# Attention block on one core: early scores moved to chunks 2 to 5, the last chunk and first step reordered, one fold behind the division, twelve idle matmuls at the start

## What is computed

```
q = Wq x + bq;  k = Wk x + bk        (32 channels each)
v = Wv x + bv                        (256 channels)
att = softmax(q^T k / sqrt(32))      (4096 x 4096)
out = gamma * (v att^T)
fused = Wf [out ; x] + bf            (1x1 convolution, 512 -> 256 channels)
```

## Time and profile before

| | us |
|---|---|
| median of 3 runs | 2091.38 |
| lowest, highest | 2089.87, 2096.21 |
| the profiled execution's own time | 2091.23 |
| its span in the trace | 2089.1 |
| PE busy in the span | 2040.8 |
| ACT busy | 1752.5 |
| DVE busy | 1589.7 |
| POOL busy | 1204.9 |

### The profile page before, as it was taken

One profiled execution on the slowest core, in us unless ns is written; L12 is line 12 of the kernel. 1 busy time (PEld: TensorE's weight loads), 2 busy tenths in 40 slices (PEclk: granted clock), 3 DMA queues, 4 the chain that ended last, 5 costly groups with the idle time before them and its releaser, 6 DMA issues.

```text
span 2089.1 us, 44966 instructions
## 1 busy us (share of the span) xinstructions
PE 2040.8 (98%) x16208; PEld 1992.9 (95%) x16208; DVE 1589.7 (76%) x2157; ACT 1752.5 (84%) x2373; POOL 1204.9 (58%) x514
## 2 busy tenths in 40 slices
PE   8899999999989999999999999999999999999999
PEld 7899999999889999999988999999998899999999
DVE  5788887886678788878666878887767778888885
ACT  6788888887788888888777888888877888888886
POOL 0376666677036766666703677666660466677665
PEclk9999999999999999999999999999999999999999
DMA  3200000000320000000031000000003100000000
GB/s 128 86 21 12 20 20 20 20 21 11 108 76 21 21 10 20 20 20 21 11 117 67 21 21 15 15 20 20 21 11 122 41 21 21 20 20 10 20 21 16
DMA packets 54081, 69.46 MB, mean 33 GB/s; under 512 B 4048, under 2 KB 37584, under 8 KB 53968
## 3 DMA queue, kind: packets, MB, share of 16 engines
q1 hardware_dynamic: 53696, 67.91, 10.0%
q10 hardware_dynamic: 272, 0.07, 0.0%
HBM read 34.41 MB, written 33.55 MB: 33 GB/s over the span
## 4 chain that ended last, share of the span: by engine, by line
PE 79%; issue 8%; DVE 7%; ACT 4%; DVEq 1%; DMA 0%; ACTq 0%; SPq 0%
PE ps_o L376 61%; PE ps_s L368 8%; PE ps_p L234 4%; DVE top L595 3%; PE ps_o L234 2%; ACT ps_p L529 2%; DVE o_norm L626 1%; PE ps_t L276 1%; ACT queries L466 1%; PE ps_t L234 1%; ACT hi L441 1%; PE ps_s L251 1%; PE ps_t L261 1%; PE ps_t L268 1%; DVE inv L622 1%
## 5 line engine op out<-in xcount | busy, mean ns | idle before, releaser
L736 POOL TENSOR_TENSOR raw<-raw,top_m 128x1024 f32<-128x1024 f32 x508 | 1204.2, 2410 | 868.0 <-ACT top_m L452 868.0
L614 DVE TENSOR_TENSOR lo<-ps_p,hi 128x1024 fp32r<-128x1024 f32 x512 | 626.9, 1224 | 329.7 <-ACT ps_p L529 319.3
L595 DVE TENSOR_TENSOR top<-ps_s,top 128x512 f32<-128x512 f32 x960 | 660.9, 688 | 69.6 <-ACT raw L447 14.5
L525 ACT ACTIVATE hi<-raw 128x1024 fp32r<-128x1024 f32 x512 | 543.9, 1062 | 176.7 <-PE ps_o L376 170.6
L376 PE MATMUL ps_o<-val_hi,hi 128*128 128x258 f32 x4096 | 673.7, 287 | 17.8 <-ACT hi L525 10.4
L376 PE MATMUL ps_o<-val_lo,hi 128*128 128x256 f32 x4096 | 654.5, 282 | 0.0
L376 PE MATMUL ps_o<-val_hi,lo 128*128 128x258 f32 x4096 | 602.0, 284 | 0.0
L447 ACT ACTIVATE raw<-ps_s 128x512 f32<-128x512 f32 x1024 | 554.2, 594 | 55.5 <-PE ps_s L368 32.5
L376 PEld LDWEIGHTS ps_o<-val_hi,hi 128*128 128x128 f32 x4096 | 564.6, 190 | 31.2 <-DVE o_norm L626 19.0
L376 PEld LDWEIGHTS ps_o<-val_lo,hi 128*128 128x128 f32 x4096 | 562.7, 190 | 0.0
L376 PEld LDWEIGHTS ps_o<-val_hi,lo 128*128 128x128 f32 x4096 | 541.4, 191 | 0.0
(11 more groups left out here) (63 smaller groups left out, 1029.9 us busy)
## 6 DMA issues: line engine op xcount, KB each, us to landing
xf<-x SPq DMA_DIRECT2D x32, 512.0 KB, 3.9
conv_d<-conv_st SPq DMA_DIRECT2D x64, 256.0 KB, 2.0
result<-conv_d SPq DMA_DIRECT2D x64, 256.0 KB, 2.6
out<-result SPq DMA_DIRECT2D x64, 256.0 KB, 2.2
raw<-wf2T SPq DMA_DIRECT2D x1, 256.0 KB, 4.3
raw<-wv SPq DMA_DIRECT2D x1, 256.0 KB, 4.1
raw<-wf1T SPq DMA_DIRECT2D x1, 256.0 KB, 4.9
raw<-wkqT ACTq DMA_DIRECT2D x1, 64.0 KB, 2.1
```

The costliest lines, as they stand in the source:

```text
L525: nc.scalar.activation(hi[:, p], raw[:, slot].rearrange("p j i -> p (j i)"), ACT.Exp, scale=SCALE).then_inc(hi_done, 1)
L595: nc.vector.tensor_tensor(top[:, new], scores, top[:, new if half else old], ALU.max).then_inc(max_done, 1)
L614: nc.vector.tensor_tensor(lo[:, t % 2], ps_p[:].rearrange("p h n -> p (h n)"), hi[:, t % 2].bitcast(F32), ALU.subtract).then_inc(lo_done, 1)
L736: nc.gpsimd.tensor_tensor(raw[:, slot], raw[:, slot], top_m[:, r].unsqueeze(1).broadcast_to((P, JQ, I)), ALU.subtract).then_inc(sub_done, 1)
```

## The change

- `BETWEEN` moves quads 8 to 11 from chunks 4 to 7 to chunks 2 to 5.
- Chunk 6: scores of quad 6 come directly after the values, then keys and queries of chunk 7, then the second convolution, on all three engines alike.
- Chunk 7: on PE the scores of quad 7 come first, then all four values, turning of the top, first convolution with the spreading in its middle, second convolution, now into a bank of `ps_s`. ScalarE copies that convolution between the exponentials of the first two steps. The exponential is cut into two functions.
- First block: step 0 has the order of the ordinary steps; scores of step 1 wait for that last convolution to be copied.
- Blocks 1 to 14: the second half of step 7's fold is done behind the division at step 0 of the next block.
- Chunk 0 of images 1 to 3: VectorE adds the convolution ahead of the low parts of keys and queries.
- Start: twelve matmuls of the 128x128 float32 identity on itself before the first wait for x, with a result that nobody reads; the first convolution of chunk 0 goes between `fold_weights` and the wait for `wvf_split`.

```diff
-    BETWEEN = {4: 8, 5: 9, 6: 10, 7: 11}
-    MADE = {q: k for k, q in enumerate((0, 1, 2, 3, 8, 4, 9, 5, 10, 6, 7, 11))}
+    BETWEEN = {2: 8, 3: 9, 4: 10, 5: 11}
+    MADE = {q: k for k, q in enumerate((0, 1, 8, 2, 9, 3, 10, 4, 11, 5, 6, 7))}
+
+    LAST_CONV = 2 * len(MADE) % BANKS + 2
...
+            def warm_up():
+
+                pe.wait_ge(id_made, 1)
+                for _ in range(12):
+                    nc.tensor.matmul(ps_t[:, 0:P], ident[:], ident[:], start=True, stop=True)
...
                 if last_chunk:
-                    project_values(0)
                     pe.wait_ge(k_out, C + 1)
+                    early_scores(c)
+                    for j in range(JC):
+                        project_values(j)
+                    turn_top(b * BLOCKS, None)
                     pe.wait_ge(q_out, C + 1)
-                    early_scores(c)
-                    project_values(1)
-                    convolve(ps_p[:, 0], 0)
-                    project_values(2)
-                    project_values(3)
-                    turn_top(b * BLOCKS, None)
-                    early_scores(BETWEEN[c])
-                    convolve(ps_p[:, 1], 1, lambda: spread_top(b * BLOCKS))
+                    convolve(ps_p[:, 0], 0, lambda: spread_top(b * BLOCKS))
+                    convolve(ps_s[:, LAST_CONV].rearrange("p j i -> p (j i)"), 1)
                     return
                 if start:
+                    warm_up()
                     pe.wait_ge(wkq_split, 1)
...
                 if start:
                     fold_weights()
+                    pe.wait_ge(wf2_split, 1)
+                    convolve(ps_t[:], 0)
                     pe.wait_ge(wvf_split, 1)
...
-                if c == CHUNKS - 2:
-                    project_kq(c + 1, C + 1)
                 if c in BETWEEN:
                     early_scores(BETWEEN[c])
-                convolve(ps_p[:, 1], 1)
-                early_scores(c)
+                if c == CHUNKS - 2:
+                    early_scores(c)
+                    project_kq(c + 1, C + 1)
+                    convolve(ps_p[:, 1], 1)
+                else:
+                    convolve(ps_p[:, 1], 1)
+                    early_scores(c)
...
+                    if first and t == 1:
+                        pe.wait_ge(conv_done, b * (2 * CHUNKS) + 2 * CHUNKS)
...
-                    if t == 0:
+                    if t == 0 and not first:
                         scores_ahead(t)
...
                 if last_chunk:
                     early_scores(c)
+                    conv_out(ps_p[:, 1], 1, C - 1)
                     values_out(0)
+                    values_out(1)
+                    keep_top(b * BLOCKS, 0)
                     conv_out(ps_p[:, 0], 0)
-                    values_out(1)
-                    early_scores(BETWEEN[c])
-                    keep_top(b * BLOCKS, 0)
-                    conv_out(ps_p[:, 1], 1)
-                    act.wait_ge(conv_done, C * 2 + 2)
                     act.wait_ge(sub0_done, b + 1)
-                    exponentials(b * STEPS, 0, 0)
+                    exponential_hi(0, 0)
+                    act.wait_ge(conv_done, C * 2 + 1)
+                    exponential(b * STEPS, 0, 0)
+                    conv_out(ps_s[:, LAST_CONV].rearrange("p j i -> p (j i)"), 1)
                     return
...
                 if last_chunk:
                     early_scores(c)
+                    reduce_top(b * HALVES + 2 * MADE[c] + 2)
                     values_lo(0)
-                    reduce_top(b * HALVES + 2 * MADE[c] + 2)
+                    reduce_turned(b * BLOCKS)
                     values_lo(1)
-                    reduce_turned(b * BLOCKS)
-                    early_scores(BETWEEN[c])
                     subtract_first(b * BLOCKS)
...
                 if finishing:
                     normalise(b * BLOCKS - 1, 1)
+                    add_conv(b * BLOCKS - 1, 0, b * (16 * USES[0]))
                 kq_lo(c, C)
                 if start:
                     setup_values()
-                if finishing:
-                    add_conv(b * BLOCKS - 1, 0, b * (16 * USES[0]))
...
                     if t == 0 and not first:
                         normalise(B - 1, 1)
+                        if not (isinstance(n, int) and n * QUADS + AHEAD > STEPS):
+
+                            fold_scores(H, AHEAD - 1, 2 * (QUADS * r + AHEAD - 1) % BANKS, 0, 0, (1,))
...
-                        fold_scores(H, t + AHEAD, 2 * (QUADS * r + t + AHEAD) % BANKS, old, 0)
+                        fold_scores(H, t + AHEAD, 2 * (QUADS * r + t + AHEAD) % BANKS, old, 0,
+                                    (0,) if t == QUADS - 1 else (0, 1))
```

More of the change, by code:

```diff
@@ L335, in project @@
                 project_values(1)
[L336 to L342, removed]
+                if not start:
+                    if finishing:
+                        pe.wait_ge(finished, b * BLOCKS)
+                    else:
+                        pe.wait_ge(conv_done, C * 2)
+                    convolve(ps_t[:], 0)
                 project_values(2)
@@ L468, in kq_hi, with conv_out @@
                     last.then_inc(q_hi_done, 1)
-                def conv_out(src, ot):
+                def conv_out(src, ot, C=C):
                     act.wait_ge(conv_ready, C * 2 + (ot + 1))
@@ L514, in project, with exponential_hi, exponential @@
                 values_out(1)
-                if c == CHUNKS - 2:
-                    kq_hi(c + 1, C + 1)
                 if c in BETWEEN:
                     early_scores(BETWEEN[c])
[L519 to L525, removed]
+                if c == CHUNKS - 2:
+                    early_scores(c)
+                    kq_hi(c + 1, C + 1)
+                else:
+                    conv_out(ps_p[:, 1], 1)
+                    early_scores(c)
+            def exponential_hi(t, slot):
+                nc.scalar.activation(hi[:, t % 2], raw[:, slot].rearrange("p j i -> p (j i)"), ACT.Exp,
                                      scale=SCALE).then_inc(hi_done, 1)
+            def exponential(Q, t, slot):
                 if not (isinstance(Q, int) and Q + t == 0):
@@ L543, in attend @@
                         act.wait_ge(sub_done, Q + (t + 2))
-                        exponentials(Q, t + 1, (QUADS * r + t + 1) % SLOTS)
+                        exponential_hi(t + 1, (QUADS * r + t + 1) % SLOTS)
+                        exponential(Q, t + 1, (QUADS * r + t + 1) % SLOTS)
                     elif not last_image:
@@ L583, in split_x, with fold_scores @@
                                         ALU.subtract).then_inc(x_split, 1)
-            def fold_scores(base, made, bank, old, new):
-                for half in range(2):
+            def fold_scores(base, made, bank, old, new, halves=(0, 1)):
+                for half in halves:
                     h = 2 * made + half
@@ L688, in project @@
                 values_lo(1)
-                if c == CHUNKS - 2:
-                    kq_lo(c + 1, C + 1)
                 if c in BETWEEN:
@@ L693, in project @@
                 early_scores(c)
+                if c == CHUNKS - 2:
+                    kq_lo(c + 1, C + 1)
             def attend(b, n, r, last_image):
```

## The result

| | before | after |
|---|---|---|
| median, us | 2090.62 (4 runs) | 2033.47 (4 runs) |
| lowest to highest | 2089.68 to 2096.21 | 2033.30 to 2033.55 |
| profiled execution, its span | 2091.23, 2089.1 | 2033.30, 2031.4 |

What follows compares the result with a forecast made beforehand. PE, busy 98%, bounds the kernel, so only its stops and half-clock time can pay. 22.4 + 6.3 + 15.5 + 10 + 3.1 = 57.3 off 2091.2 gives 2034 us, range 2027 to 2052.

Steps and rivals of the forecast that it cites:

- Fold behind the division: Blocks' step 0: PE's stop for o_norm goes, 56 x 0.40 = 22.4 us, bounds 11 to 24.
- Addition early: Chunk 0 of images 1 to 3: PE's 1.83 us wait for result goes, 6.3 us, bounds 0 to 6.3.
- behind 1.83 at the image starts in none: Starts of the three later images: the 1.83 us stop did not drop PE's clock in any.
- Chunks 2 to 7: Projection: shorter tail less work and waits handed to chunks 2 and 3, 15.5 us, bounds 8 to 18.
- first attention matmul within 1.0 us of the last convolution: End of each image's projection: sign that 1.0 us is left of PE's 2.62 us stop.
- The clock: Half-clock stretches behind projection stops go: 10 us, bounds 0 to 11.2; rival that it still drops: 2044, chance 0.12.
- some 0.3 per image comes back: Attention step 1: scores wait for a fold the slow clock hid, taking some 0.3 us per image off 11.2.
- Start: Kernel start: convolution fills the 1.69 us stop, half-clock stretch goes; 3.1 us, bounds 1.4 to 3.1, idle matmuls 0.
- the idle matmuls last longer: Rival, kernel start: 0.43 each, ending at 6.8, lifts the clock before real work; 2.6 us more, 2031, chance 0.17.
- another wait in the block: Rival, blocks: ScalarE or the fold is late, half or more of 22.4 gone, 2045 to 2056; 0.11 including a stop that stays.
- crowded chunks: Rival, four crowded chunks in a row: ScalarE's lag of some 1 us per chunk eats the tail's gain; 2050, chance 0.06.
- slower: Rival, blocks: VectorE at the division holds up half fold and subtraction, PE waits; 2095 at 1.1 us a block, chance 0.02.

Runs made afterwards that it cites:

- the table alone: Kernel before with only BETWEEN changed, quads 8 to 11 in chunks 2 to 5: 2092.8 us, ratio 0.9993.
- the two faster ones: Changed kernel with chunks 2 to 5's between-scores ahead of value 3: 2028.3 us; on top, chunk 7's keys' low part between quad 6's folds: 2027.6 us.
- the repeated kernel: The changed kernel itself, unaltered, run again as yardstick for later experiments: median 2033.8 us, ratio 0.9718 to the kernel before.

## Why the prediction was right, and where its steps were not

- **Fold behind the division: right.** 22.5 measured by undoing it, 22.4 forecast; the o_norm waits of PE are gone and come back with the order.
- **Addition early: right in the change, undersized when undone.** Chunk 0 of images 1 to 3 is 2.08 shorter each, 6.2 for 6.3. Undone alone it costs 10.1, as the clock then falls behind the stop. The step that failed is "behind 1.83 at the image starts in none", which I had read as a property of the stop; it was the case of one trace.
- **Chunks 2 to 7: 13.4 of 15.5.** 3.7 in image 0, and 3.3, 2.9 and 3.5 in the others with 2.1 and, in image 2, 1.7 of clock taken off. What was handed to chunks 2 and 3 came as forecast, 1.64 for 1.68. The mis-sized step is the tail from chunk 7's keys to attention, 10.9 by my times (68.50 to 79.4) in all images. It took 11.10 and 11.11 in images 0 and 3, where PE stands 0.97 and 0.88 by the starts, for 1.0 forecast, and what lies before that took 0.2 to 0.3 longer; and 11.62 and 11.70 in images 1 and 2, where the last stop is 1.24 and 1.30 instead of 0.80, and PE starts 0.59 and 0.64 behind the exponential's end, at the turn of the hardware loop. The prediction had nothing for that turn; it is half of the 2.1 that is missing, and its sign, "first attention matmul within 1.0 us of the last convolution", fails there. The working, step by step along the chain, was needed: by counting stops alone I put the table alone at 6.5, and it gave nothing.
- **The clock: right in direction, some 1.4 too large, and covered by a term left out.** Attention became 31.0 shorter against 30.6, but the parts differ. 22.5 are the fold. Some 1.4 are the new order of step 0 in the first block (0.7 in images 0 and 3, by its own experiment), which the prediction put at nothing. So some 7 is left for the four stretches in attention, where 8.2 was forecast; the ten idle matmuls on the kernel before show the same, 2.0 and 2.4 in images 0 and 2, which have the stretches of 6.8, where half of their busy time is 3.0 and 3.2. With the one in chunk 7 the clock gave an estimated 8.6 for the 10 forecast. My "some 0.3 per image comes back" was too little. No stop dropped the clock in the two profiles of the changed kernel (up to 1.35) and of the two faster ones (up to 1.64).
- **Start: 5.3 for 3.1.** The failing step is the price of the idle matmuls, "at least 0.21 each, so 2.6 us", and with it "I take 0". It counted records as matmuls. The eight records of 128x256 in the earlier trace rows are four matmuls (`fold_weights` issues two times two of them), and each leaves two records, so one of 256 columns takes 0.85 and one of 128 takes 0.43. The twelve took 5.49 us in the repeated kernel, all at the lower level, and 4.48 in the first trace, where the clock rose at 4.8. Either way it was up before the first real matmul, and that is worth 2.6, the upper bound given. The rival "the idle matmuls last longer" came true, mechanism and all, with the 0.43 it names. The Trainium skill ("FP8 and Floating Point Precision", TensorE Precision Notes) says that true FP32 makes four passes through the array. These traces agree, and my "row and page differ" was wrong: at the lower level the split operands' matmuls of 256 columns start 0.21 apart in the trace before, and a float32 matmul of 256 columns takes 0.85, four times that. The other parts of the 5.3 are 1.4 to 1.5 for the convolution (back in its place, chunk 1's keys start 1.5 later) and the clock's fall behind the stop of 1.69, forecast 1.7. That last part isn't certain from one execution to the next: the clock fell there in the trace before and with the table alone, but with ten idle matmuls on the kernel before, where the start is the old one too, it did not, and chunk 1's keys start at 20.58 instead of 23.15, of which some 1.2 is an earlier rise (10.1 against 12.5 us).
- The rivals that gave the gain back (another wait in the block, crowded chunks, the clock, slower) are excluded by the table and by the waits of the profile after.

The total, 2034 for 2033.5, is better than its parts: 2.2 too little at the start and 2.0 too much in the later projections cancel, and so do the clock's missing 1.4 and step 0. It was also counted from one execution of the kernel before, 2091.23. Over the later sets that kernel's median is 2093.5 to 2094.0, so the gain is nearer to 60 than to 57; the forecast of the changed kernel's own time is what held.

## What to carry to other kernels

When PE is busy 98% of the time, look at the starts of equal groups of matmuls, not at the busy share: the single largest term was 0.4 us a block that recurred 56 times, and exchanging two operations on another engine removed it. A stop of 1.5 to 2 us can cost another 1.5 us through the clock, in one image and not in the next of the same execution, so removing stops is worth more than their sum and undoing one can cost more than it showed. Before work is moved away from a wait, follow the chain that ends the wait: if the moved work isn't on it, most of the wait stays. And before a price is taken from a row's count, compare the count with the source: here one float32 matmul leaves two records.

## What was not expected of the hardware

- The turn of PE's hardware loop: with 2.4 us of filler up to the end of the pass, PE started 1.7 us after its operand was ready (601.21 to 602.91). Without filler it is 0.54 to 1.12 in the changed kernel and its variants, against 0.05 and 0.14 at the same place outside the turn.
- The clock's fall behind the same stop of 1.82 to 1.83 us: in none of three images in the profile before, in three of three in two other kernels, and in two of three in a fourth. It fell once behind 1.78 and not behind 1.97. The runs of the kernel before spread accordingly: mean granted clock 0.994 with 2089.0 us, 0.991 with 2096.7; the changed kernel's first four runs, at 1.000, spread by 0.25 us.
- A float32 matmul of 128x128 leaves two records, 0.21 us apart at the lower clock level and 0.11 at the upper (record starts in the row of the twelve), so it takes 0.43 and 0.22.
